# A graph network's two edge loops: each gather waits for the descriptors of the gather before it

## The reference, cut to what matters

```
# layer 0
all_feat = concat([x[dst], x[src], edge_attr, u], -1)
agg = segment_sum(relu(all_feat @ W1 + b1), dst)
x = layernorm(x + relu(concat([x, agg, u], -1) @ W2 + b2))
# layer 1, attention by relation
Z = einsum('ni,rio->nro', x, fc_weight)
z_s, z_d = Z[src, etype], Z[dst, etype]
e = relu(sum(concat([z_s, z_d]) * attn_weight[etype]))
alpha = softmax of e over the edges of each dst
x = layernorm(x + segment_sum(alpha * z_s, dst))
```

## Time and profile before

| what | value |
|---|---|
| time, median of 3 runs | 5511.21 us (5502.03 to 5516.64) |
| span of the profiled execution, first to last instruction | 4190.6 us |
| stretch of the layer 0 loop on Pool | 30 to 1993 us |
| stretch of the middle stage | 1993 to 2151 us |
| stretch of the layer 1 loop on Pool | 2151 to 4110 us |
| busy share of PE, DVE, ACT, Pool | 77%, 71%, 30%, 72% |
| gathers | 2 x 1563 |

### The profile page before, as it was taken

How to read it: one execution, slowest core, us unless ns; L and a number is a source line. 1 busy time by engine, 2 the same in 40 slices (tenths; PEclk the granted TensorE clock), 3 DMA queues, 4 the chain that set the end, 5 groups by cost and what they waited for, 6 DMA issues and landing times. The chain is left out here.

```text
span 4190.6 us, 74370 instructions
## 1 busy us (share of the span) xinstructions
PE 3206.3 (77%) x17849; PEld 2851.7 (68%) x17849; DVE 2985.6 (71%) x9486; ACT 1278.0 (30%) x4181; POOL 3029.9 (72%) x3265
## 2 busy tenths in 40 slices
PE   6877677777677777777857877787878888888885
PEld 6766666667666766666626767676777777777774
DVE  6876676677677777777656666676767777777777
ACT  3000000000000000000334544555555555555555
POOL 5777777777777777777257777777777777777773
PEclk6555555555555555555775555555555555555555
DMA  5322222222222222222452222222222222222221
GB/s 187 104 71 71 60 71 71 69 63 72 70 71 72 65 69 71 72 71 62 151 209 59 49 59 49 59 59 59 49 59 59 59 59 49 59 59 59 59 49 37
DMA packets 172566, 300.35 MB, mean 72 GB/s; under 512 B 71720, under 2 KB 78236, under 8 KB 158845
## 3 DMA queue, kind: packets, MB, share of 16 engines
q0 software_dynamic: 100032, 105.03, 12.7%
q1 hardware_dynamic: 43526, 104.29, 6.9%
q10 hardware_dynamic: 28598, 86.26, 6.0%
HBM read 260.36 MB, written 34.99 MB: 70 GB/s over the span
## 5 line engine op out<-in xcount | busy, mean ns | idle before, releaser
L466 POOL DMA_INDIRECT ring<-Btab,idx x1563 | 1485.5, 950 | 504.6 <-issue 338.9
L466 POOL DMA_INDIRECT ring<-Ztab,idx x1563 | 1478.9, 946 | 485.6 <-issue 352.8
L1366 PE MATMUL p_s<-ring,ohx 128*128 x3328 | 806.3, 421 | 160.5 <-issue 157.0
L1366 PEld LDWEIGHTS p_s<-ring,ohx 128*128 128x128 f32 x3328 | 734.7, 325 | 180.8 <-issue 180.8
L754 PEld LDWEIGHTS p_s<-msg,oh 128*128 128x128 f32 x3328 | 726.2, 331 | 99.8 <-issue 99.7
L754 PE MATMUL p_s<-msg,oh 128*128 128x64 f32 x3328 | 756.9, 422 | 48.4 <-ACT msg L648 45.8
L741 PE MATMUL p_m<-A,oht 128*128 x1664 | 436.1, 364 | 411.0 <-DVE full L875 401.7
L648 ACT ACTIVATE msg<-p_t 128x512 f32<-128x512 f32 x208 | 124.2, 597 | 1803.8 <-DVE p_t L881 1790.9
L746 PE MATMUL p_m<-W1c,eaT 65*128 65x128 f32 x1664 | 573.9, 449 | 24.4 <-DMA eaT<-in_eaT_in 24.4
L741 PEld LDWEIGHTS p_m<-A,oht 128*128 128x128 bf16 x1664 | 233.4, 141 | 490.4 <-issue 444.4
L1454 DVE SCALAR_TENSOR_TENSOR XA<-XA,ff,p_s 128x65 f32 x1664 | 468.4, 281 | 129.9 <-DVE XA L1454 73.1
(11 more groups left out here) (212 smaller groups left out, 3084.4 us busy)
## 6 DMA issues: line engine op xcount, KB each, us to landing
drow<-drow_d SPq DMA_DIRECT2D x53, 1024.0 KB, 5.4
drow<-drow_d ACTq DMA_DIRECT2D x51, 1024.0 KB, 5.2
eaT<-in_eaT_in ACTq DMA_DIRECT2D x208, 128.0 KB
Ztab<-Z_stage SPq DMA_DIRECT2D x49, 536.0 KB, 5.5
ring<-Btab,idx POOLq DMA_INDIRECT x1563
ring<-Ztab,idx POOLq DMA_INDIRECT x1563
xTB<-in_xTB_in SPq DMA_DIRECT2D x7, 448.0 KB, 7.7
Btab<-B_stage SPq DMA_DIRECT2D x7, 448.0 KB, 5.1
```

What stands on the lines that cost most here:

```text
L466: e.indirect_dma_start(out=ring[:, place(t), :], out_offset=None, in_=table[:, :], in_offset=bass.IndirectOffsetOnAxis(ap=idx[:, t:t + 1], ...
L1366: last = e.matmul(pS[s % 2][h][:, j % 4, :], OHx[:, s % 2, j, :], ring[:, bass.ds(t, 1), 0:D + 1], start=True, stop=True)
```

## The change

In both loops each gather gets a second semaphore, `written`, which the engine increments when it has written the gather's descriptors, beside the one that its landing increments. Before every gather but the first Pool waits until `written` has counted the gather right before it (`AHEAD` = 1). `ping`, `echo` and `echoes` go, with SP's work for them. The two consumers of `landed` copy the number that they wait for into a register of its own, by one more register instruction in each block.

```diff
-ECHO = 8
-def echoes(e, ping, echo, first):
-    for n in range(len(range(first, NT, 4))):
-        e.wait_ge(ping, n + 1).then_inc(echo, 1)
-        for k in range(ECHO - 1):
-            e.sem_inc(echo, 1)
-def gathers(e, A, ring, table, idx, s_g, landed, used, summed, ping=None, echo=None, first=NT, free={}):
+AHEAD = 1
+def gathers(e, A, ring, table, idx, s_g, landed, used, summed, written, free={}):
...
-        if j % 4 == 1 and t > first:
-            e.wait_ge(echo, ECHO * ((t - first) // 4 + 1))
+        if t >= AHEAD:
+            e.wait_ge(written, t - AHEAD + 1)
         e.indirect_dma_start(out=ring[:, place(t), :], out_offset=None, in_=table[:, :],
-                             in_offset=bass.IndirectOffsetOnAxis(ap=idx[:, t:t + 1], axis=0)).then_inc(s_g[s % len(s_g)], 16)
-        if j % 4 == 0 and t >= first:
-            e.sem_inc(ping, 1)
+                             in_offset=bass.IndirectOffsetOnAxis(ap=idx[:, t:t + 1], axis=0), engine_sem=written).then_inc(s_g[s % len(s_g)], 16)
...
-            echoes(e, S["ping"], S["echo"], EARLY)
...
             def filled(s):
-                e.wait_ge(S["landed"], e.snap(xreg[0], min_val=1, max_val=TO))
+                e.wait_ge(S["landed"], e.snap(landed, min_val=1, max_val=TO))
...
                     e.reg_load(xreg, xrow[0:1, s, :])
+                    e.reg_alu(landed, xreg[0], 0, ALU.max)
```

More of the change, by code:

```diff
@@ L486, in phase_layer0 @@
     QE, QO = 2, 3
-    EARLY = 10 * O
     H = O // 2
@@ L535, in phase_layer0 @@
         A3v = A.A3[:, 0:NB, :].rearrange("p (q h) c -> p q h c", h=2)
-        names = "oht c m0 m1 full pre msg s acc landed ping echo".split()
+        names = "oht c m0 m1 full pre msg s acc landed written".split()
         S = {n: sem("l0_" + n) for n in names}
@@ L565, in _ @@
             rows_loaded(e, A, drow, s_dr, S["oht"], 0)
-            echoes(e, S["ping"], S["echo"], EARLY)
         @block.gpsimd
         def _(e):
-            gathers(e, A, ring, A.Btab, idx, s_g, S["landed"], S["full"], S["acc"], S["ping"], S["echo"], EARLY, {XT0 // O: (T["a"], len(CHUNKS))})
+            gathers(e, A, ring, A.Btab, idx, s_g, S["landed"], S["full"], S["acc"], S["written"], {XT0 // O: (T["a"], len(CHUNKS))})
         @block.scalar
@@ L761, in _ @@
             xreg = [e.alloc_register(f"l0vx{j}") for j in range(WX)]
+            landed = e.alloc_register("l0vn")
             done = Chain(e, T["dve"])
@@ L1283, in phase_layer1 @@
         pB = [pair[1][:, 512 - 3 * O:512].rearrange("p (j c) -> p j c", c=3) for pair in p_s]
-        names = "oht e ev ohe x m3 b ed ohx s0 s acc dve ex ty landed".split()
+        names = "oht e ev ohe x m3 b ed ohx s0 s acc dve ex ty landed written".split()
         S = {n: sem("l1_" + n) for n in names}
@@ L1297, in _ @@
         def _(e):
-            gathers(e, A, ring, A.Ztab, idx, s_g, S["landed"], S["s"], S["acc"])
+            gathers(e, A, ring, A.Ztab, idx, s_g, S["landed"], S["s"], S["acc"], S["written"])
         @block.scalar
@@ L1329, in _ @@
             xreg = e.alloc_register("l1px")
+            landed = e.alloc_register("l1pn")
             def scores(s):
@@ L1334, in scores @@
                 e.reg_load(xreg, xrow[0:1, s, 0:1])
+                e.reg_alu(landed, xreg, 0, ALU.max)
                 e.wait_ge(S["oht"], s + 1)
@@ L1341, in scores @@
                     if j == 0:
-                        e.wait_ge(S["landed"], e.snap(xreg, min_val=1, max_val=TO))
+                        e.wait_ge(S["landed"], e.snap(landed, min_val=1, max_val=TO))
                     t = e.snap(treg[j], min_val=0, max_val=RING - 1)
```

## The result

The changed kernel takes 5188.8 us (median of 4 runs, 5175.6 to 5197.9), the kernel before in the same comparison 5513.0 us (median of 4, 5502.0 to 5516.6). The ratio is 0.9412, with a 95% interval of 0.9393 to 0.9431: 5.9% faster, where 3.1% slower was forecast.

A forecast was written before the change was run, and what follows sets the result against it. The prediction took Pool's gathering to bound both loops: 3126 turns of 1.731 us make 5411 us, plus 269 us outside them gives 5680 us, 3.1% slower; forecast range 5530 to 5990 us, 8-in-10 range 4550 to 6200.

The forecast's parts named there:

- The 1320.6 us: Median 5511.2 less traced span 4190.6 us, supposed to lie in both gather loops, making an ordinary turn 1.677 us.
- One turn times 3126: Both gather loops: every gather takes 0.946 + 0.04 + 0.745 = 1.731 us, 5411 us in all.
- Signal: Each gather's turn: signal from Pool's engine to its own sequencer, 0.04 us, ends 0 and 0.14.
- Release to start: Each gather's turn: from the sequencer's release to the gather's start, 0.745 us, lower end 0.40.
- Descriptors: Each gather's turn: Pool's engine writing the descriptors, 0.946 us.
- They stay behind Pool: Both loops: DVE and PE need 7.4 and 7.9 us busy per block, get one every 13.8, so Pool paces them.
- The echoes cost nothing: Layer 0's loop: echoes cost and give nothing in the trace, covered by the sequencer's 6.5 us lead.
- The register instruction: Consumers in both loops: 48 ns in each of 208 blocks, 10 us a loop, hidden in the wait for `landed`.
- The time is the span: Whole kernel: with the sequencer's lead gone, ordinary time equals the traced span, 5680 us.
- A: Gather issue in both loops is shorter than priced and the change wins, 4190 to 5490 us; chance 0.44.
- B: Whole kernel: the 1320.6 us are something else and stay, giving 7001 us; chance 0.12 with what lies between.
- C: Gather wait never bites because `written` rises when the engine takes a gather; 0.30 us gaps, 5511 us; chance 0.06.

The follow-up runs named there:

- f1: Kernel before plus only the consumers' register instruction, in a long session: 5598.1 us, ratio 1.0024 to the kernel before.
- e3: Changed kernel with the `written` wait put ahead of the ring's, so every gather carries it; short session: 4254.46 us, ratio 1.0149 to the kernel before.
- g2: Changed kernel with a second, long fulfilled wait at odd tiles, so the `written` wait stands ahead of all eight gathers; long session: 5588.8 us, ratio 1.0133 to before.
- f2: The changed kernel itself, run again in a long session: 5418.2 us, ratio 0.9709 to the kernel before.
- g1: The changed kernel itself, in another long session: 5195.3 us, ratio 0.9426 to the kernel before.
- g4: Changed kernel without signal and wait in layer 1, so the change is in layer 0 alone; long session: 5211.1 us, ratio 0.9450 to the kernel before.
- e2: Kernel before without ping and echo, with the register instruction added; short session: 4191.43 us, ratio 1.0000 to the kernel before.
- m2: Kernel before without ping and echo, with the register instruction added; long session: 5674.0 us, ratio 1.0138 to the kernel before.
- f3: Changed kernel with the `written` wait put ahead of the ring's, so every gather carries it; long session: 5810.5 us, ratio 1.0415 to the kernel before.
- h2: Changed kernel with a second, fulfilled wait at every second gather also in early blocks, from the third; long session: 5212.7 us, ratio 0.9357 to the kernel before.
- h1: The changed kernel itself, in a long session: 5409.5 us, ratio 0.9709 to the kernel before.
- e4: Changed kernel with `AHEAD` = 8, so it waits for the eighth gather before; short session: 4191.24 us, ratio 0.9999 to the kernel before.
- e1: Kernel before plus only the consumers' register instruction, in a short session: 4191.05 us, ratio 0.9999 to the kernel before.

## Why the prediction was wrong, step by step

Two steps failed. The sum for the time priced a gap of 0.785 us at all 3126 gathers, where 1696 of them have 0.30. And the time that it was set against was taken for Pool's own pace, where other engines hold Pool up in a long session, and do so less when its gaps are longer. By the first step alone the span would have been 4838 us, an estimate worked out at the end of this section; it is 5196, and the other 358 us are the second step.

**The 1320.6 us.** "Spread over 3126 gathers", 1.677 us a gather in an ordinary run: called a supposition, and this is the second step, the one that took the sign with it. Such a turn exists (1.678 in f1's layer 0; that it is so near is luck, since layer 1's is 1.493 and some 250 us more lie in the middle and at the end), but it isn't a longer gather with its gap. It is a gather of 0.95 us, a gap of 0.30, and now and then a stop of 3 to 5 us for an engine that is slow while gathers run. Since I took 1.677 for Pool's own pace, I set it against 1.731 and had 170 us for the sign. The right comparison was Pool's own 1.25 before, with some 1260 us of stops on top, against a Pool with a longer turn and few stops.

**"One turn times 3126".** The size of the turn was right where it applies. Signal: 0.034 us for the 0.04. Release to start: 0.713 for 0.745. Descriptors: 0.945 for 0.946. A gap of 0.75 lies in the forecast's 0.74 to 0.89. But it applies to 683 gaps of layer 0 and as many of layer 1, and 855 and 841 are 0.30. The sentence "in all three the wait was an instruction of its own ahead of the gather, where now it is the gather's own, so it may come out a little shorter" had the question and the wrong size: not a little, but all of 0.45 us. Which of two waits is attached follows from the order in which they are written (e3). By the Trainium skill, page "Perfetto Trace Analysis", section "DMA Instruction — SWDGE (GPSIMD)", an instruction is decoded and queued before its semaphores hold; for a gather that carries its wait the trace agrees (0.30 us), and for a wait that stands ahead of it the trace shows 0.75. For the kernel that has the turn everywhere, g2, the sum nearly holds: a span of 5597 us for the 5680, its loops 2666 and 2650 for 2705 each. In layer 0, gaps of 0.748 and not 0.785 us make 54 us less and 98 gaps that are still short 44 less, while 27 stops (16 of 3.1 us, the others of 1.0 to 1.1) and a gather of 961 ns give 64 back. g2 is 1.3% over the kernel before, so the kernel that I priced is a loss; that the sign fits is partly luck, since the price was set against a supposed turn.

**"They stay behind Pool".** Largely right in layer 0 of the compared run, where 535.1 of DVE's 630.0 us end with `landed`; in the slower long sessions DVE ends the layer 21 instructions behind (f2), as it does in f1. Wrong in layer 1: 4.8 of PE's 109.3 us. Pool's 1.492 us there are its own gaps (behind the first 184 gathers, all but 7 us of g1's stops are the regular long gaps told of below), and PE falls behind it: a step of PE takes 11.5 us with the waits (g1) and 11.8 without (g4), and 11 and 17 steps are left at Pool's last gather. A step has 7.5 us of busy time by the earlier trace rows (1551.4/208), and takes 7.6 after the last gather, so some 4 us a step are neither work nor Pool, and weren't in any row of a short session.

**"The echoes cost nothing".** Right in the short session (e2), wrong in the long one, where their absence costs 1.4% (m2). The register instruction costs nothing in the short one, at most 0.24% in the long.

**"The time is the span".** Right within 2 us, but not because the lead went: it holds for the kernel with the lead as well (f1, 5598.1 and 5596.3).

**The rivals.** A (the issue is hidden, the change wins; 0.28 for 4900 to 5490) gave the sign, and its mechanism is real for half of the gathers. Its path to the time is wrong all the same: where all of the issue is hidden, as in f3, the kernel is 4% slower than before, not at 4602. B fell with the two times, and C with the 0.75 us gaps. No case had what happens: that a slower Pool makes the others faster.

**What stays open.** Shown is, for long sessions, that the other engines take 1.6 to 1.9 times as long for a step while gathers follow at 0.30 us gaps as after the last gather, that gaps of 0.75 us at every second gather take part of this from layer 0 (13.7 us a step in f3, 12.0 in f2), and that with 0.75 us at all of them Pool never stops for the others (g2), whose own pace can't be seen then. Not shown is why. The long register instructions are only its visible part: f3 and m2 have fewer of them on DVE than f1 (120 and 133 to 447) and are slower, and PE's pauses shown above stand beside no register instruction of such a length. Whether the writing of descriptors and the sequencers of the other engines share something wasn't tested.

Nor is it known what makes a session short or long; by the record's numbers the short session and the last long one, with 5599 us, were on the same chip, so the chip alone doesn't decide it. The changed kernel took 5189 and 5195 us in two sessions and 5409 to 5432 in five others. By the first trace of the changed kernel and that of f2 the difference, 219 us in all, lies in the middle (161 and 291 us), the end (162 and 195), layer 1 (2413 and 2452) and layer 0 (2430 and 2447). The middle has no gathers, but most of it is again what layer 0 left: 3 instructions of DVE on the ring in the one (14 us) and 21 in the other (146 us). So in five sessions DVE is slower beside the gathers than Pool's new turn and in two it isn't, and why is open too.

In a short session, where Pool sets the pace, I would expect Pool's own turn, (1.250 + 1.695)/2 = 1.473 us behind the first 184 gathers of each loop (1.487 with the rare long gaps below) and 1.27 in them: 2 x (1379 x 1.487 + 234) + 269 = 4838 us, 15% slower than before. That is an estimate from the rows; it wasn't run.

## What to carry to other kernels

Read time and span of the same execution before making a theory of their difference; if they are of different runs, the difference may be another regime, in which other engines bound the kernel. When a wait is added to an instruction that has one already, look which of the two is attached and which becomes an instruction ahead: here the one written last becomes the instruction ahead, that was 0.45 us a gather, and in a long session it decided the sign (f2 against f3). And where Pool writes descriptors back to back and other engines are slower beside it than after its last gather, try a pace: h2 is 6.4% faster than the kernel before, and 3.6% faster than h1, by waiting more.

## What the runs showed of the hardware

- A gather that carries its wait for the one before starts 0.30 us after that one's end, no later than without a wait (e3); one with the wait as an instruction ahead starts 0.75 us after it, 0.71 after the release.
- Pool's signal reaches its own sequencer 0.034 us after the gather's end (683 times in layer 0 of the changed kernel).
- In a long session DVE takes 13.4 us from one of its instructions on the ring to the next beside gathers with gaps of 0.30 us and 7.3 after the last one (f1), with 48 and 55 GB/s moved.
- Register and semaphore instructions of DVE's and SP's sequencers, 17 to 84 ns otherwise, take 0.7 or 1.4 us in stretches of layer 0 of a long session while gathers follow at 0.30 us gaps (f1).
- With the wait for the gather right before, one gap in 96 is mostly 1.6 us (e3, f3), 1.9 us (changed) or 3.1 us (g2), each time before the same gathers of a loop (113, 209, 305 and so on, counted from 0), in both kinds of session. The kernel before has none, and neither has e4 with the signal but a lead of eight; their cause wasn't looked for.
- One kernel's time differs by a third between sessions, 4192 and 5513 to 5599 us, and is steady within each. The granted clock was 0.50 in a stretch of either kind (1180 to 1300 us of e1 and of f1).
